# Layer norm emitted one tile ahead, and the input loads moved to two other queues, in an 8-core macaron block kernel

## The reference

```python
x = x + 0.5 * _L0_ffn_ref(_layernorm(x), G1_R, G2_R, G1_I, G2_I, bias_real, bias_imag)
x = x + _L0_attn_ref(_layernorm(x), Wq, Wk, Wv, Wo, Wg, Wb, cq_w, cq_b, ck_w, ck_b, cv_w, cv_b)
x = x + 0.5 * _L0_ffn_ref(_layernorm(x), G1_R, G2_R, G1_I, G2_I, bias_real, bias_imag)

def _layernorm(x, axis=-1, eps=1e-5):
    m = jnp.mean(x, axis=axis, keepdims=True)
    v = jnp.var(x, axis=axis, keepdims=True)
    return (x - m) / jnp.sqrt(v + eps)

def _unfold_tt(G1, G2):
    W = jnp.einsum('abcd,cefg->abefdg', G1, G2)
    return W.reshape(OUT_FEATURES, IN_FEATURES)      # 512 x 512, real and imaginary
```

## Time and profile before

| | |
|---|---|
| time, median of 2 runs | 4136.53 us (4134.75 and 4138.32) |
| the profiled execution, its own time | 4142.7 us |
| its span on the slowest core (core 6) | 4141.1 us |
| spans of the 8 cores | 4097.8 to 4141.1 us |
| mean granted TensorE clock, each core | 0.558 to 0.560 |
| busy: PE, DVE, ACT | 1251.4, 1398.6, 407.7 us |

### The profile page before, as it was taken

The page is one execution under the profiler, slowest core; times in us unless marked ns, Lnnn a source line. Parts: engine busy times, 40 slices in busy tenths (PEclk is TensorE's granted clock), DMA queues, the critical chain, the costliest instruction groups (busy, mean ns, idle before and its releaser), DMA issues.

```text
span 4141.1 us, 35564 instructions; the slowest of 8 cores (4097.8 to 4141.1 us)
## 1 busy us (share of the span) xinstructions
PE 1251.4 (30%) x12064; PEld 619.5 (15%) x12112; DVE 1398.6 (34%) x2799; ACT 407.7 (10%) x1129; POOL 164.0 (4%) x222
## 2 busy tenths in 40 slices
PE   0453313321133333112333321033333211332253
PEld 0111101111121111112120111032111111211111
DVE  1222113455431244554122445532134554212121
ACT  0224300011000001110000011000000110000121
POOL 0000000000100000001000000100000001000000
PEclk9765655555555555555555555555555555555576
DMA  4001202200812221018213210901222008122002
GB/s 123 3 0 26 56 8 42 26 12 9 23 21 41 41 31 21 9 10 19 36 26 51 25 19 9 25 12 31 43 39 26 12 9 22 21 41 46 16 1 81
DMA packets 296322, 114.94 MB, mean 28 GB/s; under 512 B 215568, under 2 KB 273056, under 8 KB 296128
## 3 DMA queue, kind: packets, MB, share of 16 engines
q0 software_dynamic: 136240, 63.04, 19.2%
q1 hardware_dynamic: 136864, 45.81, 4.5%
q10 hardware_dynamic: 23040, 3.81, 0.5%
HBM read 147.46 MB, written 26.08 MB: 42 GB/s over the span
## 4 chain that ended last, share of the span: by engine, by line
PE 29%; DVE 25%; DMA 22%; issue 11%; ACT 7%; SPq 2%; ACTq 1%; DVEq 1%; POOL 1%; POOLq 0%
PE pp L251 29%; DMA wring<-woT 8%; DMA wring<-wqT 2%; DMA wring<-wkT 2%; DMA wring<-wvT 2%; SPq L274 2%; DVE subtmp L921 2%; ACT xln L399 1%; DMA scr_tc<-tcst 1%; DMA lgT<-scr_flat 1%; ACTq L274 1%; ACT cacc L632 1%; DVE cacc L928 1%; ACT xTt L435 1%; DVE cacc L635 1%
## 5 line engine op out<-in xcount | busy, mean ns | idle before, releaser
L251 PE MATMUL pp<-x2s,wring 128*128 128x512 bf16 x752 | 334.5, 620 | 587.1 <-DMA wring<-wqT 110.4
L251 PE MATMUL pp<-wring,oT 128*128 128x512 bf16 x240 | 113.3, 622 | 397.0 <-DMA wring<-woT 397.0
L251 PEld LDWEIGHTS pp<-x2s,wring 128*128 128x128 bf16 x768 | 98.4, 137 | 822.5 <-issue 822.5
L623 DVE COPY rawt<-pp 128x512 f32<-128x512 f32 x96 | 66.3, 691 | 404.0 <-PE pp L251 404.0
L251 PE MATMUL pp<-ci,xln 128*128 128x128 bf16 x384 | 81.3, 271 | 384.8 <-ACT xln L399 330.3
L1198 DVE TENSOR_TENSOR R<-R,pp 128x512 f32<-128x512 f32 x32 | 20.5, 683 | 479.3 <-PE pp L251 479.3
L251 PE MATMUL pp<-big,xTt 128*128 128x512 bf16 x496 | 174.2, 512 | 25.5 <-ACT xTt L435 24.8
L632 ACT ACTIVATE cacc<-rawt,cconvb,cconvw 128x512 f32<-128x512 f32 x96 | 78.0, 813 | 1052.0 <-DVE rawt L623 1052.0
L251 PE MATMUL pp<-stripB,stripA 16*16 16x16 bf16 x2048 | 53.9, 167 | 356.7 <-DMA stripB<-scr_t16t 307.0
L459 DVE SCALAR_TENSOR_TENSOR R<-pp,R 128x512 f32<-128x512 f32 x64 | 44.3, 692 | 343.2 <-PE pp L251 343.2
L1147 ACT ACTIVATE Sb<-Sm 128x512 bf16<-128x512 f32 x32 | 20.1, 629 | 1357.5 <-DVE Sm L1144 1357.5
(11 more groups left out here) (152 smaller groups left out, 2426.4 us busy)
## 6 DMA issues: line engine op xcount, KB each, us to landing
wring<-woT POOLq DMA_DIRECT2D x64, 512.0 KB, 5.3
R<-x SPq DMA_DIRECT2D x16, 512.0 KB, 15.9
x2s<-scr_x2t SPq DMA_DIRECT2D x8, 1024.0 KB, 6.7
wring<-wqT POOLq DMA_DIRECT2D x16, 512.0 KB, 5.6
wring<-wkT POOLq DMA_DIRECT2D x16, 512.0 KB, 5.7
wring<-wvT POOLq DMA_DIRECT2D x16, 512.0 KB, 5.6
out<-R SPq DMA_DIRECT2D x16, 512.0 KB, 6.7
scr_w<-wb SPq DMA_DIRECT2D x8, 512.0 KB, 2.6
```

The costliest lines, as they stand in the source:

```text
L251: return e.matmul(out, lhsT, rhs, start=start, stop=stop, tile_position=tp)
L623: e_raw = self.dve(lambda e, pb=pb: e.tensor_copy(self.rawt[:, 3:3 + 512], pb[:, 0:512]), deps=(ev_last,))
```

## The change

The 16 loads of x leave QS. They are issued behind the factors, tiles of even number on QG and tiles of odd number on QA, so QS starts with the constants. ev_cs is now the arrival of the constants alone; ev_cg is taken before the loads of x and stays the arrival of the bias, gate weights and factors. In both loops with a layer norm, _emit_ln for tile i+1 is now emitted before the transposes of tile i; that of tile 0 stands before the loop. _emit_ln, the buffers and every operation are the same as before. (A branch for a debug setting, MK.SUB >= 10, moves with it and is not taken.)

```diff
     def p0_loads(self):
         xr = self.x_in.rearrange("(n p) m -> n p m", p=128)
-        self.ev_R = [self.dma(QS, self.Rt[i][:], xr[i]) for i in range(NTT)]
...
         self.ev_cs = self.s.now(QS)
         self.dma(QG, self.c_fbias[:], self.fbias)
+        self.ev_R = None
...
         self.ev_cg = self.s.now(QG)
+        self.ev_R = [self.dma((QG, QA)[i % 2], self.Rt[i][:], xr[i])
+                     for i in range(NTT)]
...
     def p_ln_ffn(self, which):
-        for i in range(min(NTT, MK.NTILES)):
+        nt = min(NTT, MK.NTILES)
+
+        def emit_tile_ln(i):
             par = i % 2
             extra = list(pre) + ([self.ev_R[i]] if which == 1 else [])
...
-            else:
-                ev_ap = self._emit_ln(i, par, extra)
+            return self._emit_ln(i, par, extra)
+
+        ap_pend = {0: emit_tile_ln(0)} if nt else {}
+        for i in range(nt):
+            par = i % 2
+            ev_ap = ap_pend.pop(i)
+            if i + 1 < nt:
+                ap_pend[i + 1] = emit_tile_ln(i + 1)
...
     def p3_ln2(self):
+        ap_pend = {0: self._emit_ln(0, 0, (self.ev_ffn[0],))}
         for i in range(NTT):
             par = i % 2
-            ev_ap = self._emit_ln(i, par, (self.ev_ffn[i],))
+            ev_ap = ap_pend.pop(i)
+            if i + 1 < NTT:
+                ap_pend[i + 1] = self._emit_ln(i + 1, (i + 1) % 2,
+                                               (self.ev_ffn[i + 1],))
```

More of the change, by code:

```diff
@@ L420, in p_ln_ffn @@
             if MK.SUB >= 10:
-                ev_ap = self.act(lambda e, i=i, par=par: e.activation(
+                return self.act(lambda e, i=i, par=par: e.activation(
                     self.xln[par][:], self.Rt[i][:], AF.Copy), deps=extra)
-            else:
-                ev_ap = self._emit_ln(i, par, extra)
+            return self._emit_ln(i, par, extra)
[5 more added lines that the diff above has]
+                ap_pend[i + 1] = emit_tile_ln(i + 1)
             if sub < 2:
```

## The result

The changed kernel takes 4084.4 us (median of 7 runs, 4082.8 to 4096.0) beside 4136.6 for the kernel before (6 runs on the same chip). The ratio is 0.9879, with a 95% interval of 0.9866 to 0.9891: 50 us or 1.2% faster. The forecast was 45 us, 4091.5. The profiled execution took 4088.5 us; its slowest core is core 5.

What follows compares the result with a forecast made beforehand. No engine near full, the kernel was taken as a chain of waits; 13 (opening) + 11.3 + 9.3 + 11.3 = 44.9, say 45 us, off the 4136.5 median gave 4091.5 us, range 4075 to 4108, 8 in 10 for 4068 to 4124.

Steps and rivals of the forecast that it cites:

- That is the old chain with another tile's layer norm in it: Feed-forward: in-order DVE and ACT keep a layer norm in each tile's chain; only the first transpose leaves it.
- Rival A: Feed-forwards: the layer norm really leaves the path, 5.0 us saved for each of 15 tiles, 168 us, 3968; 3 in 100.
- The gain of 0.60 per tile from addition to first eviction: Feed-forward tiles 1 to 14: first eviction 1.14 us after the normalizing activation starts instead of 1.74; 8.4 us per feed-forward.
- The last tile: End of each feed-forward: nothing is normalized in front of its evictions, so 5.0 us are saved.
- the second layer norm: Second layer norm stage: the first transposes leave ACT's chain; 8.4 plus 3.0 less 2.1, a gain of 9.3 us.
- The sign it set, 14.3 us per tile: Feed-forward in the profile after: a tile should take 14.3 us instead of 14.9.
- The feed-forwards' terms, 11.3 each: Each feed-forward gains 8.4 + 5.0 - 2.1 = 11.3 us from the layer norm one tile ahead, twice: 22.6.
- Rival B: Feed-forwards: moved transposes make TensorE's clock rise too late; 48 us lost, 45 gained, 4139.5, slower; 5 in 100.
- The opening's term, 13 us: Opening: factors and first write of scr_w come earlier, 17.6 us, less 4 for contention; gain 13, between -8 and 28.
- the contention with the writes, costed at 4 us: Opening: POOL's half of x beside the four scr_w writes; bytes of three of them waiting for x cost 4 us.
- Rival C: Opening gives nothing: x from two queues is as much in the way; 24 us in all, 4112.5; 17 in 100.
- the prediction's issue term: Opening: by the skill's rule alone, spreading loads saves only issue time, 38.73 - 33.7 = 5 us, less contention.

## Why the prediction was right, and where it was not

- "That is the old chain with another tile's layer norm in it": right. The timeline shows the chain, and moving the emission behind the evictions shows that the order was its cause: 218.6 to 139.1 us per feed-forward. Rival A was wrong for the change, for the reason given, and describes what that other order does (4.5 us per tile from the chain, and more where the clock stays up).
- The gain of 0.60 per tile from addition to first eviction: right (5.29 to 4.69). The last tile and the second layer norm (10.2 for 9.3) too. The sign it set, 14.3 us per tile, was not met: the tiles took 13.65.
- The feed-forwards' terms, 11.3 each, were too small by 8 and 7 us. The step that failed is the unspoken one that the matmuls of a tile take after the change what they took before. The mean tile of 14.9 us held slow second halves that come from the tile's length against the clock; at 13.65 they vanish. Rival B looked at the right place and at the wrong side: it let the clock cost 48 us when the transposes move, and the clock gave about 15. The two runs with an added Ln show that the place of the transposes is not what matters.
- The opening's term, 13 us, measured 4.3. Three of its steps were too kind. It started from core 6, whose first write came at 38.7 where the median of the cores is 36.0. The factors landed at 24.6 and not 19, since ACT's half of x took until 20 us and not 15, and POOL's own x moved beside the factors and not only behind them. And the contention with the writes, costed at 4 us, took 7 in the first write alone (9.8 for 2.7), with the reads no sooner than 50.8 (42 by the forecast's own steps). The wrong idea in it was that small transfers lose only a share beside large ones: with x waiting for the writes, the first small reads waited for all of x. Rival C, 4112.5, had the mechanism; its terms were taken at their worst and the truth lay between.
- The two errors, -9 and +15, partly cancel, so that a forecast off by 5 to 7 us in 50 had terms off by more. That the sum came out so near is luck; the mechanism of the layer norms is not.

By the Trainium skill, "DMA: Bandwidth & Descriptors", section "Issuing engines are not separate DMA queues", spreading loads over issuing engines saves no more than issue time. The run with the loads alone agrees: the opening gained 2.7 us by the stage medians, no more than the 5 us of the prediction's issue term. The small loads did gain a place, as the prediction said (first matmul at 8.4 when x waits for them), but what they gained was paid for behind them.

## What to carry to other kernels

Emitting a step one tile earlier takes it off the path only if, on each in-order engine it uses, it stands in front of what waits for the matmuls and behind what the matmuls wait for; read the order on both engines before believing the code. A transfer that is wanted late is best kept away from a chain of small dependent transfers, in whatever queue: here moving it to a stage in which the DMA engines idle gained 14 us, and moving it between queues or within the stage gained 4 at most. And where the clock rises and falls within a loop's body, a change in the body's length changes its matmuls too: bound that in both directions.

## What the runs showed of the hardware that was not expected

A loop of fixed work can hold its place against the clock's rise: tiles of 13.6 to 13.8 us over a whole stage with a half of 2.15 us in each, whereas tiles that would be 0.4 us longer creep and fall out every fifth time at 15.3. Windows of the changed kernel's second feed-forward, core 0, cut where the granted clock changes:

```profile
3885.04:3891.87 6.83, 3.02 (x14) 1.00 (x12) 3.10 (x7) 0.86 (x3) 0.00 (x0) 1.00 0.00 0
3891.87:3898.69 6.82, 3.93 (x13) 1.67 (x14) 0.00 (x0) 2.55 (x9) 0.00 (x0) 0.50 0.00 0
3898.69:3905.52 6.83, 3.04 (x14) 0.99 (x12) 3.10 (x7) 0.85 (x3) 0.00 (x0) 1.00 0.01 1
```

There is one stretch at full and one at half clock in every tile, and from one rise to the next it is as long as the tile, 13.65 us; so each rise meets the same matmuls. What sets the length of such a stretch no run here shows.

In the second feed-forward of the changed kernel cores 4 and 5 were slower than the others, 231.4 and 230.4 us against 219 to 220.5. Nearly all of their second halves took 2.57 us or more, and the window of core 4 shows why:

```profile
3890.00:3893.00 3.00, 1.78 (x8) 0.49 (x6) 1.35 (x3) 0.00 (x0) 0.00 (x0) 0.81 0.00 0
```

The granted clock was 0.81 in the second half of a tile, where core 6 had 1.00 in the same window. The tiles of cores 4 and 5 were then 14.0 to 15.4 us, in the drifting pattern again; cores 6 and 7 show the same 2.57 in their last three tiles only. By the Trainium skill, "TensorE: Matmul & The Clock Gate", section "Seeing it yourself", a current limiter grants 13/16 of the clock once three cores of a die run dense matmuls. The figure agrees (0.81). The condition is not borne out as simply: all 8 cores did the same work, two cores of one die had it through most of the stage, its other two only at the end, and the other die not at all. Nor does that level appear in any of the eleven other traces, which hold the same or denser matmuls on all cores. What set it off no run here shows.
